# Re-ordering the double step of two attention stages: scores and weighted sum first on TensorE, both output projections last

## The reference

```python
def _attn(x, ctx, Wq, Wk, Wv, Wo, bo):          # 16 heads of 64
    q, k, v = x @ Wq, ctx @ Wk, ctx @ Wv         # each cut into heads
    attn = softmax(einsum("bihd,bjhd->bhij", q, k) * 64 ** -0.5)
    return einsum("bhij,bjhd->bihd", attn, v).reshape(b, n, 1024) @ Wo + bo
h = _ln(x, g1, be1); x = _attn(h, h, Wq1, Wk1, Wv1, Wo1, bo1) + x
h = _ln(x, g2, be2); x = _attn(h, context, Wq2, Wk2, Wv2, Wo2, bo2) + x
h = _ln(x, g3, be3); a, gate = split(h @ Wp + bp)
x = a * gelu(gate) @ W2 + b2 + x
```

## Time and profile before

| | us |
|---|---|
| median of 3 runs (lowest, highest) | 3159.14 (3155.99, 3168.3) |
| profiled execution, its own time | 3161.7 |
| its span | 3159.9 |
| PE busy | 2997.0 (95% of the span) |
| DVE, ACT, POOL busy | 2302.1, 1879.8, 1407.4 |

### The profile page before, as it was taken

One profiled execution on the slowest core, in us unless ns is written; L12 is line 12 of the kernel. 1 busy time (PEld: TensorE's weight loads), 2 busy tenths in 40 slices (PEclk: granted clock), 3 DMA queues, 4 the chain that ended last, 5 costly groups with the idle time before them and its releaser, 6 DMA issues. The chain is left out here.

```text
span 3159.9 us, 77497 instructions
## 1 busy us (share of the span) xinstructions
PE 2997.0 (95%) x25600; PEld 2595.8 (82%) x25600; DVE 2302.1 (73%) x3851; ACT 1879.8 (59%) x5615; POOL 1407.4 (45%) x977
## 2 busy tenths in 40 slices
PE   7999999999999998699999999999999969999999
PEld 6888888888888887588888888888888758888888
DVE  6777777777777776587788777878887755555654
ACT  6666666666666665466666666666666632322232
POOL 5555555555555554455555555555555420001100
PEclk9999999999999999899999999999999989999999
DMA  8777788778787777588888878888888750000000
GB/s 253 235 236 234 233 239 236 233 236 242 237 240 238 236 239 225 173 241 240 239 243 248 240 238 240 242 241 244 240 244 239 229 145 27 27 27 33 33 27 21
DMA packets 464424, 625.01 MB, mean 198 GB/s; under 512 B 57728, under 2 KB 397056, under 8 KB 464128
## 3 DMA queue, kind: packets, MB, share of 16 engines
q1 hardware_dynamic: 460256, 624.09, 66.2%
q10 hardware_dynamic: 4128, 0.41, 0.1%
HBM read 330.71 MB, written 293.60 MB: 198 GB/s over the span
## 5 line engine op out<-in xcount | busy, mean ns | idle before, releaser
L382 POOL TENSOR_TENSOR self_probs<-self_probs,self_row_inv 128x1024 f32<-128x1024 f32 x256 | 484.8, 1894 | 578.2 <-DVE self_row_inv L576 575.4
L382 POOL TENSOR_TENSOR cross_probs<-cross_probs,cross_row_inv 128x1024 f32<-128x1024 f32 x256 | 484.8, 1894 | 565.3 <-DVE cross_row_inv L576 565.3
L429 ACT ACTIVATE cross_probs<-cross_ps_s,cross_neg_max 128x256 f32<-128x256 f32 x1024 | 474.5, 472 | 198.3 <-DVE cross_blocks L568 134.2
L429 ACT ACTIVATE self_probs<-self_ps_s,self_neg_max 128x256 f32<-128x256 f32 x1024 | 474.4, 472 | 121.8 <-DVE self_blocks L568 76.6
L549 DVE TENSOR_REDUCE self_neg_max<-self_ps_s 128x2 f32<-128x512 f32 x512 | 328.8, 684 | 170.2 <-PE self_ps_s L719 170.2
L549 DVE TENSOR_REDUCE cross_neg_max<-cross_ps_s 128x2 f32<-128x512 f32 x512 | 331.6, 684 | 135.0 <-PE cross_ps_s L719 134.0
L568 DVE STREAM_TRANSPOSE cross_blocks<-cross_probs 128x1024 f32<-128x1024 f32 x256 | 315.4, 1232 | 10.3 <-DMA cross_turns<-cross_blocks 9.4
L568 DVE STREAM_TRANSPOSE self_blocks<-self_probs 128x1024 f32<-128x1024 f32 x256 | 315.0, 1231 | 1.0 <-POOL self_probs L382 1.0
L738 PE MATMUL self_ps_o<-self_probs_t,self_v 128*64 128x256 f32 x2048 | 258.3, 388 | 30.4 <-DMA self_probs_t<-self_turns 30.2
L738 PE MATMUL cross_ps_o<-cross_probs_t,cross_v 128*64 128x256 f32 x2048 | 257.7, 389 | 27.2 <-DMA cross_probs_t<-cross_turns 26.8
L481 ACT ACTIVATE self_qk_hi<-self_ps_qk 128x512 fp32r<-128x512 f32 x256 | 153.2, 599 | 213.4 <-PE self_ps_s L719 114.3
(11 more groups left out here) (170 smaller groups left out, 9623.8 us busy)
## 6 DMA issues: line engine op xcount, KB each, us to landing
self_turns<-self_blocks SPq DMA_DIRECT2D x1024, 128.0 KB, 2.8
self_probs_t<-self_turns SPq DMA_DIRECT2D x256, 512.0 KB, 4.3
cross_turns<-cross_blocks SPq DMA_DIRECT2D x1024, 128.0 KB, 2.9
cross_probs_t<-cross_turns SPq DMA_DIRECT2D x256, 512.0 KB, 4.3
self_xt<-in_x SPq DMA_DIRECT2D x32, 256.0 KB, 6.3
self_xres<-in_x SPq DMA_DIRECT2D x32, 256.0 KB, 2.7
after_self_attention<-yout SPq DMA_DIRECT2D x32, 256.0 KB, 2.4
cross_xt<-after_self_attention SPq DMA_DIRECT2D x32, 256.0 KB, 6.4
```

Source lines behind the costliest of these rows:

```text
L382: pool.tensor_tensor(tile, tile, scale, ALU.mult).then_inc(probs_ready, 1)
L429: last = act.activation(probs[:, slot % 2, h, t], scores[:, slot % 2, h, t], ACT.Exp, bias=neg_max[:, slot % 2, i:i + 1], accum_out=row_su ...
```

## The change

It shifts the lags and the order in the double step on all five engines.

- PE: two scores (pairs p - 2 and p - 1) and two weighted sums (p - 8 and p - 7) come first, then project_qk(p), project_v, project_qk(p + 1), and two project_out last. In a step with a turn (self: p = 6; cross: p = 4 and 6) the turn and both project_out stand between the two project_qk, and project_v is last.
- SP: the loads of p - 6 and p - 5 stay at the head of the step, which now lies a double step ahead of their use. The store of an odd pair (p - 3) comes before that of the even one (p - 2). The store of y and the residual's load move from p = 6 to p = 2, with y a sequence later.
- DVE and ACT: the even pair's maxima, exps and turn all lie in one step, the odd pair's turn in the next. `copy_v` moves to the head of the next step. `output` moves to p = 0.
- POOL: the low parts of h and context move from p = 6 of the sequence before to p = 0, ahead of the normalising; the 64 rows of the context's low part move from DVE to POOL; the layer norm moves from p = 2 to p = 4 and the residual from p = 0 to p = 6.
- `sequences` unrolls two sequences ahead of the loop, and one more step behind the drain.

```diff
-SCORES, EXPS, NORMED, TURNED, LOADED, WEIGHTED, PROJECTED = 1, 2, 3, 4, 6, 6, 8
+SCORES, EXPS, NORMED, TURNED_EVEN, TURNED_ODD, LOADED, WEIGHTED, PROJECTED, SUMMED = 2, 2, 2, 2, 4, 6, 8, 8, 16
...
-TURN_CONTEXT, TURN_H = 2, 4
+TURN_CONTEXT, TURN_H = 4, 6
...
 def sequences(nc, eng, n, step):
-    for p in range(0, PAIRS, 2):
-        step(0, p, FIRST)
-    with nc.Fori(1, n - 1, engines=[eng.engine], hint_back_edge=True) as b:
+    for b in range(2):
+        for p in range(0, PAIRS, 2):
+            step(b, p, FIRST)
+    with nc.Fori(2, n - 1, engines=[eng.engine], hint_back_edge=True) as b:
         for p in range(0, PAIRS, 2):
             step(b, p, LOOP)
     for p in range(0, PAIRS, 2):
         step(n - 1, p, LAST)
     for p in range(0, PROJECTED, 2):
         step(n, p, DRAIN)
+    step(n + 1, 0, DRAIN)
...
+        def live(part, b, p, lag):
+            if part == FIRST:
+                return PAIRS * b + p >= lag
+            return PAIRS * (b - n) + p < lag if part == DRAIN else True
...
+            def load_turn(b, p, part):
                 slot = (p - LOADED) % PAIRS
+                if part == DRAIN:
+                    sp.wait_ge(pv_done, PAIRS * b + p - LOADED - RING + 1)
                 sp.wait_ge(turn_stored[slot % 2], stored_count(b, p - LOADED))
                 sp.dma_start(probs_t[:, slot % RING], turns[slot].rearrange("j k i n -> (j k) (i n)")
                              ).then_inc(turn_loaded[slot % RING], 16)
             def step(b, p, part):
                 for pair in (p, p + 1):
-                    if alive(part, pair, LOADED):
-                        load_turn(b, pair)
+                    if live(part, b, pair, LOADED):
+                        load_turn(b, pair, part)
                 if part in (FIRST, LOOP) and p == 0:
                     load_next(b + 1)
-                for pair in (p, p + 1):
-                    if alive(part, pair, TURNED):
-                        store_turn(b, pair)
-                if part == FIRST and p == 2:
+                if p == 2 and live(part, b, p, SUMMED):
+                    store(b - 2)
+                    sp.wait_ge(y_stored, 16 * (b - 1))
+                    load_residual(b - 1)
+                if live(part, b, p + 1, TURNED_ODD):
+                    store_turn(b, p + 1, TURNED_ODD)
+                if live(part, b, p, TURNED_EVEN):
+                    store_turn(b, p, TURNED_EVEN)
+                if part == FIRST and b == 0 and p == 2:
                     prefetch(sp)
-                if part in (LOOP, LAST) and p == 6:
-                    store(b - 1)
-                    sp.wait_ge(y_stored, 16 * b)
-                    load_residual(b)
...
                 pool.tensor_tensor(c_lo[:], c_t[:, 0], c_hi[:, 0].bitcast(F32), ALU.subtract).then_inc(c_ready, 1)
+                pool.wait_ge(c_ready, 2 * b + 1)
+                pool.tensor_tensor(c_hi[64:P, 1], c_t[64:P, 1], c_hi[64:P, 1].bitcast(F32),
+                                   ALU.subtract).then_inc(c_ready, 1)
+                pool.wait_ge(c_ready, 2 * b + 2)
...
             def step(b, p, part):
-                for pair in (p, p + 1):
-                    if alive(part, pair, NORMED):
-                        normalise(b, pair)
-                if part != FIRST and p == 0:
-                    residual(b - 1)
-                if part in (FIRST, LOOP) and p == 2:
+                if part != DRAIN and p == 0 and counts(b):
+                    low_h(b)
+                    if cross:
+                        low_context(b)
+                if part in (FIRST, LOOP) and p == 4:
                     norm_power(b + 1)
                     norm_apply(b + 1)
-                if part in (FIRST, LOOP) and p == 6:
-                    low_h(b + 1)
-                    if cross:
-                        low_context(b + 1)
+                if p == 6 and live(part, b, p, PROJECTED):
+                    residual(b - 1)
+                for pair in (p, p + 1):
+                    if live(part, b, pair, NORMED):
+                        normalise(b, pair)
...
             def step(b, p, part):
                 g = PAIRS * b + p
-                if alive(part, p, PROJECTED):
+                even, odd = (p - EXPS) % RING, (p + 1 - EXPS) % RING
+                if p == 0 and counts(b) and part != DRAIN:
+                    high_h(b)
+                    if cross:
+                        high_context(b)
+                elif part != DRAIN and p > 0:
+                    copy_v(b, p - 2)
+                if live(part, b, p, EXPS):
+                    exps(g - EXPS, even, 0)
+                if p == 0 and live(part, b, p, EXPS):
+                    copy_v(b - 1, 6)
+                if live(part, b, p, EXPS):
+                    exps(g - EXPS, even, 1)
+                if live(part, b, p, PROJECTED):
                     high_o(b, p)
                 if part != DRAIN:
                     high_parts(g, p)
-                if alive(part, p, EXPS):
+                if part in (FIRST, LOOP) and p == TURN_H:
+                    scale_shift(b + 1)
+                if live(part, b, p + 1, EXPS):
                     for h in range(2):
-                        exps(g - EXPS, (p - EXPS) % RING, h)
+                        exps(g + 1 - EXPS, odd, h)
                 if part != DRAIN:
-                    copy_v(b, p)
-                    if part in (FIRST, LOOP) and p == TURN_H:
-                        scale_shift(b + 1)
-                    if part in (FIRST, LOOP) and p == 6:
-                        high_h(b + 1)
-                        if cross:
-                            high_context(b + 1)
                     high_parts(g + 1, p + 1)
-                if alive(part, p + 1, EXPS):
-                    for h in range(2):
-                        exps(g + 1 - EXPS, (p + 1 - EXPS) % RING, h)
...
             def step(b, p, part):
                 g = PAIRS * b + p
-                if alive(part, p, NORMED):
+                if live(part, b, p, SCORES):
+                    for h in range(2):
+                        maxima(g - SCORES, 0, h)
+                if live(part, b, p + 1, TURNED_ODD):
+                    turn(b, p + 1, TURNED_ODD)
+                if live(part, b, p, SCORES):
+                    maxima(g + 1 - SCORES, 1, 0)
                     inverse(b, p)
-                if alive(part, p, PROJECTED):
+                    maxima(g + 1 - SCORES, 1, 1)
+                if p == 0 and live(part, b, p, SUMMED):
+                    output(b - 2)
+                if live(part, b, p, PROJECTED):
                     low_o(b, p)
-                if alive(part, p, TURNED):
-                    turn(b, p)
                 if part != DRAIN:
                     low_parts(g, p)
-                if part != FIRST and p == 6:
-                    output(b - 1)
-                if alive(part, p + 1, TURNED):
-                    turn(b, p + 1)
-                if alive(part, p + 1, NORMED):
+                if part in (FIRST, LOOP) and p == TURN_CONTEXT and cross:
+                    context_copy(b + 1)
+                if live(part, b, p, TURNED_EVEN):
+                    turn(b, p, TURNED_EVEN)
+                if live(part, b, p, SCORES):
                     inverse(b, p + 1)
                 if part in (FIRST, LOOP) and p == 2:
                     norm_stats(b + 1)
-                if alive(part, p, SCORES):
-                    maxima(g - SCORES, (p - SCORES) % 2, 0)
                 if part != DRAIN:
                     low_parts(g + 1, p + 1)
-                if part in (FIRST, LOOP) and p == TURN_CONTEXT and cross:
-                    context_copy(b + 1)
-                if alive(part, p, SCORES):
-                    maxima(g - SCORES, (p - SCORES) % 2, 1)
-                if part in (FIRST, LOOP) and p == 6 and cross:
-                    low_context(b + 1)
-                if alive(part, p + 1, SCORES):
-                    for h in range(2):
-                        maxima(g + 1 - SCORES, (p + 1 - SCORES) % 2, h)
...
-                if cross and part in (FIRST, LOOP) and p == TURN_CONTEXT + 2:
+                if cross and part in (FIRST, LOOP) and p == TURN_CONTEXT:
                     pe.wait_ge(c_t_ready, b + 2)
-                if part in (FIRST, LOOP) and p == TURN_H + 2:
+                if part in (FIRST, LOOP) and p == TURN_H:
                     pe.wait_ge(h_t_ready, b + 2)
...
             def weigh(b, p):
                 q = (p - WEIGHTED) % PAIRS
-                seq = b if p >= WEIGHTED else b - 1
-                pe.wait_ge(v_ready, PAIRS // 2 * seq + q // 2 + 1)
-                if counts(c := PAIRS // 2 * b + (p - WEIGHTED) // 2):
-                    pe.wait_ge(o_ready, c)
+                pe.wait_ge(v_ready, PAIRS // 2 * (b - 1) + q // 2 + 1)
                 slot = (p - WEIGHTED) % RING
...
             def step(b, p, part):
+                for pair in (p, p + 1):
+                    if live(part, b, pair, SCORES):
```

(58 more changed lines are left out.)

## The result

The changed kernel takes 3210.92 us in the median (3207.2 to 3213.69, 4 runs) beside 3158.57 for the kernel before: a ratio of 1.0159 (95% interval 1.0135 to 1.0183). It is slower by 52 us, where 45 us faster was forecast, and outside the range. Its profiled execution spans 3211.9 us.

What follows compares the result with a forecast made beforehand. PE's list was taken to set the time in both attentions. From 3161.7 us, removed waits take 108, project_qk stalls add 73 and the ends take 10: 3117 profiled, 3114 for a median, range 3071 to 3145.

Steps and rivals of the forecast that it cites:

- The step that failed: SP at p = 2: stores and y's wait, behind the loads, are covered by a double step (9 us).
- The sum: Whole kernel: 3161.7 - 108 + 73 - 10 = 3117 us profiled, 3114 for a median.
- the load wait: PE waiting for loads of `probs_t`, 57 us (30.2 in self, 26.8 in cross): gone in both stages.
- the turns' wait for `copy_v`: PE's turns in cross behind `copy_v` on ACT, 16.7 us: gone.
- the wait for the context's low part: PE's project_qk behind the context's low part on POOL, 11.0 us: gone unless POOL is late.
- The stall at project_qk: project_qk(p + 1) on PE waits for ACT and DVE: 0.27 us each in self, 0.51 in cross, 73 us in all.
- the clean sum: PE's time for a sequence without waits: 37.94 us in self, 36.32 in cross.
- The ends: Drains and first sequences: -5 us a stage, -10 in all; bounds -8 and +3 a stage.
- The DVE rival: DVE late for project_qk's low part, its odd turn delayed by POOL or exps: 3192 us at 0.5 us; 10%.
- POOL at p = 0: Rival in cross: POOL's low parts and normalising come late, 0.6 us a sequence, 19 us: 3133; 14%.
- Both outer cases: Rivals outside the range: small or no project_qk stalls, 3041 us (8%), and DVE late, 3192 us (10%).
- the load case: Rival: PE's load wait stays, loads queueing behind stores in bursts; 57 us return, 3171 us; 8%.

Runs made afterwards that it cites:

- Experiment 1: Changed kernel with y's store at p = 2 behind both stores of turns, its wait and the residual's load at p = 4: 3140.07 us, 0.9933.
- experiment 2: Changed kernel with y's store ahead of the two loads: 3141.18 us; with y's store, wait and residual's load behind both turns' stores: 3151.28 us.
- experiment 7: Kernel before with y's wait and residual's load at p = 0 of the next sequence: 3098.34 us; with only its second sequence unrolled: 3164.59 us.
- experiments 4 and 5: Changed kernel with the next stage's weights loaded ahead of the first store of turns: 3191.45 us; with y's store and wait moved too: 3122.07 us.
- c1_y_prefetch: Changed kernel with y's store behind the turns' stores, its wait at p = 4, and weights' loads ahead of the first store of turns: 3122.07 us, 0.9870.
- c2_before_y: Kernel before with the wait for y's store and the residual's load at p = 0 of the next sequence, second sequence unrolled: 3098.34 us, 0.9796.
- the split alone: Changed kernel with one project_out between project_v and project_qk(p + 1), the other behind it, in steps without a turn: 3229.91 us, 1.0222.

## Why the prediction was wrong, point by point

**The step that failed** is this sentence on SP: "What follows it on SP (stores, the wait for y's store at p = 2) now has that double step as cover". It holds for the loads, which are ahead of the wait, and not for the stores of turns, which are behind it. Those stores free `blocks` for DVE's next turn of the same parity, one double step later, and that turn stands near the head of DVE's step, with `low_o` behind it. The sum asks only what the loads need: it has no term for who waits for what stands behind the wait, nor for y's store landing later (6.3 us, before 2.4) because two loads of 512 KB are now issued just ahead of it. Experiment 1 puts the price at 71 us, and experiment 2 gets 60 and 70 of them back by order alone.

**The second omission** is the weights' loads, "the longer unrolled code can cost instruction loads" being the only cost that I allowed in the first sequences. An unrolled sequence costs nothing that can be measured (experiment 7); the weights' loads, held back by the first store of turns and issued right in front of the next ones, cost 18 to 19 us (experiments 4 and 5).

Together they make up the miss: 3114 + 71 + 19 = 3204, measured 3211. With both mended the kernel stands at 3122, 8 us over the forecast; by its ratio, 0.9870 x 3158.57 = 3118, it is 4 over.

**What was right.** The waits removed: between the first and the last turn of a stage the load wait, the turns' wait for `copy_v` and the wait for the context's low part are gone from PE's list. The stall at project_qk is there with its terms. In cross at p = 2:

```profile
1580.16 0.28 PE L680 MATMUL cross_ps_misc<-cross_lo_wv,cross_c_hi 128*128 128x256 f32 x1
...
1580.70 0.38 PE L664 MATMUL cross_ps_qk<-cross_h_hi,cross_hi_wq 128*128 128x256 f32 x1 [0.27 <-DVE cross_qk_lo L572]
...
1580.92 0.28 PE L664 MATMUL cross_ps_qk<-cross_h_hi,cross_lo_wq 128*128 128x256 f32 x1
...
1579.32 0.60 ACT L496 ACTIVATE cross_qk_hi<-cross_ps_qk 128x512 fp32r<-128x512 f32 x1 [0.88 <-PE cross_ps_qk L664]
...
1579.95 0.69 DVE L572 TENSOR_TENSOR cross_qk_lo<-cross_ps_qk,cross_qk_hi 128x512 fp32r<-128x512 f32 x1 [0.44 <-ACT cross_qk_hi L496]
```

The next matmul behind the last of project_v would have come at 1580.28; it came at 1580.70, and the one after it 0.22 later: 0.42 + 0.10, forecast 0.51. The periods in c1_y_prefetch are 38.83 for 39.05 and 37.98 for 37.64. Its PE timeline shows the stalls, taken in the same way. In self the next project_qk comes at 985.13 where 984.69 was due (p = 0), at 994.75 for 994.59 and at 1004.37 for 1004.21 (p = 2 and 4): 0.54 + 0.26 + 0.26 = 1.06 us with the 0.10 each, forecast 1.11. The profile lists only the first of them as a wait, so its count in self is 32 and not 96. Most of what is left of the 0.22 in self is the clean sum, 37.94, which is too long: c2_before_y runs at 37.82 a sequence. In cross the stall at p = 0 is 0.93 (1831.00 for 1830.17) where 0.51 + 0.3 was forecast; that is 0.12 of the 0.34, and some 0.2 stay open.

**The ends** were forecast at -10 us. By its ratio c1_y_prefetch is 1.3% or 41 us faster than the kernel before; (38.73 - 38.83 + 39.14 - 37.98) x 30 = 32 of them are periods, so some 9 lie in the ends. The number is right once the weights' loads are out of the way, but nothing here shows that it is made up as forecast: the -5 us a stage were taken from 2.7 us of moved work, and this agreement may be luck. The block on SP also cost some 9 us in the drain of self (experiment 1), where the sum had a gain.

**The rivals.** The mechanism that decided was in none of them. The DVE rival has the right victim, DVE's odd turn late and `low_o` behind it, and the wrong cause: I named POOL or the exps, and excluded it by POOL's slack. POOL at p = 0 cost 2.7 us in one wait in the first sequence of cross and nothing in the steady part. And the earlier trace rows misled me on what the change was for: the load waits came from the same block on SP (the wait for y's store at p = 6, in front of the next step's loads), as experiment 7 shows, not from a distance too short. The chances have a slip of their own: "Both outer cases stay outside, under 2 in 10" leaves out the load case, whose 3171 also lies outside the range; the three have 8 + 10 + 8 = 26%.

## What to carry to other kernels

When a step is moved on a queue that both issues DMAs and waits, list what stands behind it and when each of those is needed, and what stands ahead of it in the same queue: here 1 MB of loads issued just ahead took the landing of a 256 KB store from 2.6 to 6.3 us. Before lengthening a pipeline because a consumer waits for a load, look at when that load was issued and what held its queue: here moving one wait gave more (66 us) than the new order with the same kind of repair (42 us). An edit that helps (one project_out on each side) can lose while another bottleneck is in place and win once it is gone, so undo parts together as well as one at a time.

## What the hardware showed that I had not expected

A store of 256 KB issued by SP right behind two loads of 512 KB landed in 6.3 us, the same store ahead of them in 2.6. In the split alone the granted clock fell from 1.00 to 0.50 some 0.9 us after PE had stood idle for 2.34 us and taken up work again, once a sequence, and stayed there for about 3 us (mean 0.96 over 1500 to 1800); behind gaps of 1.40 us in the changed kernel it stayed at 1.00. What else in those steps took part in the fall is not separated here.
